# Graph-attention edge pass: VectorE's own semaphore against drains between its dependent instructions

## The reference

```python
def gat_layer(h, src, dst, W, al, ar, b):
    feat = (h @ W).reshape(n, H, F)                  # H = 4 heads, F = 64
    el = jnp.sum(feat * al[None], axis=-1)
    er = jnp.sum(feat * ar[None], axis=-1)
    e = jax.nn.leaky_relu(el[src] + er[dst], 0.2)
    m = jax.ops.segment_max(e, dst, num_segments=n)
    ex = jnp.exp(e - m[dst])
    denom = jax.ops.segment_sum(ex, dst, num_segments=n)
    a = ex / denom[dst]
    msg = feat[src] * a[:, :, None]
    out = jax.ops.segment_sum(msg, dst, num_segments=n)
    out = out + b.reshape(1, H, F)
    return jax.nn.elu(out).reshape(n, H * F)
```

## Time and profile before

| | |
|---|---|
| median of 3 runs | 8269.03 us (8267.43 to 8291.18) |
| the profiled execution | 8222.85 us |
| its span, first to last instruction | 8220.9 us |
| VectorE busy | 5315.2 us (65%), 9727 instructions |
| GpSimd busy | 5491.2 us (67%), 5324 instructions |
| ScalarE busy | 2245.6 us (27%) |
| TensorE matmuls busy | 2470.7 us (30%), almost none of it in `gat_edges` |

### The profile page before, as it was taken

How to read it: one execution, slowest core, us unless ns; L and a number is a source line. 1 busy time by engine, 2 the same in 40 slices (tenths; PEclk the granted TensorE clock), 3 DMA queues, 4 the chain that set the end, 5 groups by cost and what they waited for, 6 DMA issues and landing times. The chain is left out here.

```text
span 8220.9 us, 58166 instructions
## 1 busy us (share of the span) xinstructions
PE 2470.7 (30%) x11337; PEld 1689.0 (21%) x11337; DVE 5315.2 (65%) x9727; ACT 2245.6 (27%) x5114; POOL 5491.2 (67%) x5324
## 2 busy tenths in 40 slices
PE   4777777777667676000000000005100000000000
PEld 4444444444444455000000000004000000000000
DVE  6777777777768777556556655663456556655666
ACT  3667666767667552000000000002000000000002
POOL 4777777767777646666666666647766666666664
PEclk8888988888888798555555555557555555555555
DMA  7555555555555547555555555543455555555556
GB/s 240 162 167 164 167 163 167 168 160 170 160 160 168 157 135 217 166 189 196 184 197 179 201 180 198 185 170 93 140 191 190 191 195 182 197 182 200 176 207 220
DMA packets 680849, 1466.14 MB, mean 178 GB/s; under 512 B 164313, under 2 KB 497566, under 8 KB 667420
## 3 DMA queue, kind: packets, MB, share of 16 engines
q0 software_dynamic: 250192, 671.13, 28.1%
q1 hardware_dynamic: 430540, 793.82, 27.2%
HBM read 752.61 MB, written 713.36 MB: 178 GB/s over the span
## 5 line engine op out<-in xcount | busy, mean ns | idle before, releaser
L1810 POOL DMA_INDIRECT gb_g<-table,ix_g x3126 | 2965.2, 949 | 1442.6 <-issue 938.1
L585 POOL DMA_INDIRECT gb<-table,src x1563 | 1897.1, 1214 | 679.5 <-issue 468.9
L1910 DVE SCALAR_TENSOR_TENSOR gb_g<-gb_g,same_g,wv 128x256 f32<-128x256 f32 x3024 | 1450.0, 479 | 1135.8 <-DVE gb_g L1910 471.3
L1096 PE MATMUL pm<-ident,tl 128*4 128x128 f32 x2 | 0.7, 372 | 4531.2 <-DMA tl<-sums 4531.2
L619 PE MATMUL po<-parts,sel 128*128 128x256 f32 x3930 | 1026.0, 411 | 501.3 <-ACT ost L685 353.5
L1837 ACT ACTIVATE ww<-ee 128x132 f32<-128x132 f32 (+3 forms) x102 | 28.5, 280 | 4030.2 <-DVE ee L1888 2811.7
L1898 DVE TENSOR_TENSOR wv<-gb_g,ww 128x1024 f32<-128x1024 f32 x782 | 955.2, 1221 | 0.0
L1096 PEld LDWEIGHTS pm<-ident,tl 128*4 128x4 f32 x2 | 0.2, 81 | 4532.1 <-DMA tl<-sums 4532.1
L619 PEld LDWEIGHTS po<-parts,sel 128*128 128x128 f32 x3930 | 762.8, 202 | 746.5 <-issue 478.1
L762 DVE TENSOR_TENSOR pt<-gb,pt 128x256 f32<-128x256 f32 x392 | 175.8, 449 | 546.4 <-ACT pt L679 414.8
L679 ACT ACTIVATE pt<-pt,sh 128x128 f32<-128x128 f32 x1568 | 436.8, 344 | 331.8 <-remote 175.2
(11 more groups left out here) (302 smaller groups left out, 4208.3 us busy)
## 6 DMA issues: line engine op xcount, KB each, us to landing
sums<-gb_g SPq DMA_DIRECT2D x94, 4224.0 KB
sums<-ost SPq DMA_DIRECT2D x393, 512.0 KB
gb_g<-table,ix_g POOLq DMA_INDIRECT x3126
gb<-table,src POOLq DMA_INDIRECT x1563
table<-f SPq DMA_DIRECT2D x48, 520.0 KB
x<-in_x SPq DMA_DIRECT2D x50, 256.0 KB
at<-in_rbf SPq DMA_DIRECT2D x100, 128.0 KB
hT_d<-hT SPq DMA_DIRECT2D x49, 256.0 KB
```

The costliest lines, as they stand in the source:

```text
L585: eng.indirect_dma_start(out=gb[:, group(k), half(k) + j, 0:4, :].rearrange("p a c -> p (a c)"), out_offset=None, in_=q.table0[:, :], in_o ...
L1810: eng.indirect_dma_start(out=gb[:, p, j, 0:FR], out_offset=None, in_=q.table1[:, :], in_offset=bass.IndirectOffsetOnAxis(ap=ix[:, s * SBT ...
L1910: ins = eng.scalar_tensor_tensor(rows[:, t0 + t, 0:D], row, same[:, t:t + 1], wv[k % 2][:, j, :], ALU.mult, ALU.add)
```

## The change

`s_dv`, `own`, `after` and the clearing are gone. Where VectorE waited for its own count, it now has a `drain()`: an instruction of VectorE's sequencer that holds what follows until VectorE's earlier instructions are done. The wait for its own last row sum at a superblock's top becomes a drain too. All waits for other engines and for DMAs stay, and so do the updates that other engines wait for (`s_d`, `s_den`, `s_sum`).

```diff
-        s_dv = q.sem(nm("dv"))
...
-                def body(s, p, t0, t1, first, masks, arrived, before, behind, m_before):
+                def body(s, p, t0, t1, first, masks, arrived, behind, m_before):
                     m = t1 - t0
-                    made = 0
-
-                    def own(ins):
-                        nonlocal made
-                        made += 1
-                        ins.then_inc(s_dv, 1)
-                        return made
-
-                    def after(k):
-                        eng.wait_ge(s_dv, k)
-
...
-                    eng.wait_ge(s_sum.sem, before)
-                    eng.nop(nofuse=True)
-                    eng.sem_clear(s_dv)
+                    eng.drain()
                     eng.tensor_copy(same[:, 0:m], q.samep[:, here])
                     eng.wait_ge(s_seg.sem, s_seg.at(s, back=1))
                     eng.tensor_copy(lead(ee), carry(mm_))
                     eng.wait_ge(*arrived)
-                    k_el = own(eng.tensor_tensor(x, rows[:, t0:t1, D:FR].rearrange("p t h -> p h t"), held[:, :, here], ALU.add))
-                    after(k_el)
-                    k_el = own(eng.scalar_tensor_tensor(x, x, 0.2, x, ALU.mult, ALU.max))
-                    after(k_el)
-                    k_fs = own(eng.tensor_tensor_scan(line(fs, m), add_m, line(ee, m), -BIG, ALU.add, ALU.max))
-                    after(k_fs)
-                    k_mm = own(eng.tensor_tensor_scan(line(mm_, m)[:, ::-1], back_m, line(fs, m)[:, ::-1], -BIG, ALU.add, ALU.max))
-                    after(k_mm)
+                    eng.tensor_tensor(x, rows[:, t0:t1, D:FR].rearrange("p t h -> p h t"), held[:, :, here], ALU.add)
+                    eng.drain()
+                    eng.scalar_tensor_tensor(x, x, 0.2, x, ALU.mult, ALU.max)
+                    eng.drain()
+                    eng.tensor_tensor_scan(line(fs, m), add_m, line(ee, m), -BIG, ALU.add, ALU.max)
+                    eng.drain()
+                    eng.tensor_tensor_scan(line(mm_, m)[:, ::-1], back_m, line(fs, m)[:, ::-1], -BIG, ALU.add, ALU.max)
+                    eng.drain()
                     eng.tensor_tensor(heads(ee, m), heads(ee, m), heads(mm_, m), ALU.subtract).then_inc(s_d.sem, 1)
...
-                    k_w = own(weighted(0))
-                    after(k_w)
-                    k_dn = own(eng.tensor_tensor(lead(ww), lead(ww), carry(dn), ALU.mult))
-                    after(k_dn)
+                    weighted(0)
+                    eng.drain()
+                    eng.tensor_tensor(lead(ww), lead(ww), carry(dn), ALU.mult)
+                    eng.drain()
                     eng.tensor_tensor_scan(line(dn, m), mul_m, line(ww, m), 0.0, ALU.mult, ALU.add).then_inc(s_den.sem, 1)
-                    k_row = k_w
                     for t in range(m):
                         k, j = divmod(t, 4)
                         row = acc[:, :] if t == 0 else rows[:, t0 + t - 1, 0:D]
-                        after(k_row)
+                        eng.drain()
                         ins = eng.scalar_tensor_tensor(rows[:, t0 + t, 0:D], row, same[:, t:t + 1], wv[k % 2][:, j, :], ALU.mult, ALU.add)
                         if t == m - 1:
                             ins.then_inc(s_sum.sem, min(2, len(quads(t0, t1))))
-                        else:
-                            k_row = own(ins)
```

More of the change, by code:

```diff
@@ L1947, in whole @@
                     body(s, p, 0, SBT, s * SBT, [y[:, bass.ds(s * (H * W), H * W)] for y in (q.seg_add, q.seg_back, q.seg_mul)],
-                         (s_g[p].sem, s_g[p].at(i)), s_sum.at(s, 0), gb[:, (p - 1) % B, SBT - 1, 0:D], SBT)
+                         (s_g[p].sem, s_g[p].at(i)), gb[:, (p - 1) % B, SBT - 1, 0:D], SBT)
                 with eng.Fori(0, LOOPS) as i:
@@ L1958, in _ @@
                     body(SB - 2 + x, p, t0, t1, s * SBT + t0, [y[:, :] for y in end_masks[x]],
-                         (s_ge[x], 16 * (t1 - t0)), summed(x),
+                         (s_ge[x], 16 * (t1 - t0)),
                          gb[:, p, t0 - 1, 0:D] if t0 else gb[:, (p - 1) % B, SBT - 1, 0:D], ENDS[x - 1][2] - ENDS[x - 1][1] if x else SBT)
```

## The result

| | before | after |
|---|---|---|
| median of 4 runs each, on one chip | 8270.01 us (8267.43 to 8291.18) | 8440.61 us (8438.23 to 8449.05) |
| the profiled execution | 8222.85 us | 8440.26 us |
| from the first gather of a pass to its last row sum | 2250.4, 2248.2 us | 2338.2, 2340.7 us |

The ratio is 1.0207, 95% interval 1.0185 to 1.0228: the change makes the kernel **slower by some 170 us**. The forecast was 7715 us. The two passes alone are 88 + 92 = 180 us longer; the other 37 us between the two profiled executions lie ahead of them, in stages that the change doesn't touch (the profiled execution of before was the short one).

What follows compares the result with a forecast made beforehand. VectorE, at 44.9 us a superblock against GpSimd's 40.0, was taken as the bound. 8222.85 - 504 (GpSimd's waits) - 44 (the passes' ends) = 7675 us, put at 7715 for the median of the runs; range 7640 to 8030.

Steps and rivals of the forecast that it cites:

- GpSimd's 40.0 us: Edge passes: GpSimd needs 32 x 1.25 = 40.0 us a superblock when nobody holds it, and becomes the bound.
- VectorE's 28.9 us a clean superblock: Edge passes: VectorE would take 28.9 us a superblock with no late waits, which cost it 16 us.
- `wv` starts on time while dependents are late: VectorE's late regime: `wv`, which waits for nothing, starts on time; row sums stand 1.40 us apart, 0.92 us idle.
- The drains' own price: VectorE: 39 drains a superblock, a 0.12 us gap behind each in place of 0.035, add 4.2 us a superblock.
- the 33.1 of the sum: VectorE's superblock without late waits but with the drains' cost of 4.2 us added: 33.1 us.
- If what is late is the semaphore alone, all waits for itself are on time again: VectorE's waits for `s_dv`: a drain waits for earlier instructions, not a semaphore, so its 16 us a superblock of lateness largely go.
- the term - 504 us: Both edge passes: GpSimd's waits for VectorE's `wv`, 253.6 + 250.9 us, go.
- rival C: VectorE: completion itself is late and a drain sees it no sooner; + 200 to + 390 us, about 8550; chance 0.10.
- not under 400: Expected sign in the changed profile: VectorE's idle time before row sums falls from 1079 us to under 400.
- Its instructions end as before: VectorE's late regime: the engine isn't slow, row sums still last 0.48 us; only news of an end comes late.
- So VectorE sets the pace: Edge passes: VectorE bounds them at 44.9 us a superblock, since GpSimd waits for it and it hardly waits for gathers.
- C's boundary of 0.41 us a drain: If completion itself is late, the change loses above 16 us / 39 = 0.41 us a drain over today's good gap.

Runs made afterwards that it cites:

- the paced kernel: Kernel before, with a 128-column GpSimd memset behind each gather that first waits for the memset before it: 8251.78 us against 8309.21; repeated on another chip, ratio 0.9891.
- the paced kernel with drains: Changed kernel with a 128-column GpSimd memset behind each gather that first waits for the memset before it: 8260.84 us (kernel before, same chip: 8309.21).
- the paced kernels: A waiting GpSimd memset behind each gather: 16 or 128 columns in the kernel before, 128 in the changed one: 8263.46, 8251.78 and 8260.84 us against 8309.21.
- the first experiment: Changed kernel, each row sum reading `acc` and not the row before it, 23 of 32 drains ahead of row sums removed: 8416.44 us (kernel before: 8289.66).
- The kernel with breaks: Kernel before, with eight GpSimd memsets of 1500 columns behind every 16 gathers of the whole superblocks: 9903.21 us (kernel before, same chip: 8309.21).

## Why the prediction was wrong

*What held.* GpSimd's 40.0 us, VectorE's 28.9 us a clean superblock (a superblock of the paced kernel: 42.9 us from top to top, less 14.0 of waiting for gathers, is 28.9), and that `wv` starts on time while dependents are late. The drains' own price was taken too high: 31.4 us a superblock in the paced kernel with drains (45.6 less 14.2 of waiting) against the 33.1 of the sum. Had the late waits gone, VectorE would have had even more room than I gave it.

*The step that failed* is "If what is late is the semaphore alone, all waits for itself are on time again", and with it the term - 504 us. The condition was false. A drain lets go no sooner than a semaphore does, as rival C said: behind drains the late row sums stand 1.40 us apart, VectorE's idle time before them is 1105.5 us, not under 400, and GpSimd's waits grew by 79 and 84 us a pass in place of going. "Its instructions end as before" was read off a record of durations and an instruction that had nothing to wait for, and neither says when a wait learns that an instruction has ended. I had noted that `wv` doesn't rule this out and gave C 0.10 all the same, on one drain in a good stretch. A drain of 0.1 us there says nothing on a late stretch.

*A deeper step failed too:* "So VectorE sets the pace". Its lateness has a cause in GpSimd's gathers: without half of them, or with breaks in them, it is gone. Late stretches begin 29 to 43 us after GpSimd takes up its run of 64 gathers (median 33) and end mostly 6 to 10 us after it stops for a buffer, before the change and after it. As I read it, the two engines hold each other: gathers at 1.25 us make VectorE late, VectorE late keeps a buffer, GpSimd stops, and VectorE catches up. So to remove late waits is not to gain them: the paced kernels have lost most of their late row sums and still take 2225 to 2235 us a pass, at the 1.41 us a gather that the kernel before has on average too. The 40.0 us a superblock at which the prediction put GpSimd were never reached over a whole pass.

*Rival C's size.* It had + 200 to + 390 us and 8550; measured were + 170. It priced a superblock at 4.2 us more, where the drains add 2.5, and it let half the late steps swallow it. In fact all do: a late quad takes 7.00 us with or without drains. What is left for the drains is the good stretch. There VectorE falls behind, and GpSimd's stop lasts until it has caught up, 11.0 us becoming 14.4 on average: 23 stops x 3.4 = 78 us a pass, and the tail behind the last gather takes 52.7 us for 45.8. That is 85 of the 90 us. The 85 us are measured; that the longer good quad is why the stops grew is argued, from the table above, and the kernel with fewer drains speaks against its being the only reason. C's boundary of 0.41 us a drain had no meaning, since the late waits came back at any price.

*The rule* of the Trainium skill that I had weighed, in VectorE: DVE Perf Modes, on the drain that can't be avoided, says that a semaphore after each instruction costs nothing extra. By it nothing was to be gained from giving up `s_dv`, and I had added that the drains could only cost. That pointed to the right side. But the trace disagrees with its reason, in good stretches too: row sums that wait for nothing (the first experiment) take 1.25 us for three, 0.39 us apart, those behind a semaphore stand 0.52 us apart, and those behind a drain 0.555.

*Left open:* what holds a gather to 1.40 us, and how that makes a VectorE instruction's end late in steps of 0.70 us. It is not the stores, not the bytes, and not the gathers' data, which land in time. That the late time goes with the number of instructions, and that GpSimd's memsets are late too, points at something that the engines share when an instruction ends.

One candidate is the recording itself. Each gather adds 16 to its semaphore, and the trace should have an event for each. Just after GpSimd resumes it has 79 for 8 gathers (before, 4326 to 4336 us), in the late stretch behind it (4350 to 4400) 36 for 40. The kernel with breaks, which is hardly ever late, has some 300 for 30 throughout. So late stretches are those in which the trace loses most such events. Either the updates are in each other's way on the chip, or the profiler, which writes them down, slows the engines. The narrower gathers have as many updates as the full ones, so they don't tell. No execution without recording and no kernel with fewer updates at the same run of gathers is on record, so it isn't known whether these stretches are there when nobody records.

Open too are the waits of 3.7 to 4.5 us at a superblock's top. In each run that has them the queue of kind instruction moved 1.25 to 1.93 MB (1.34 in the changed kernel), in each other one 0.73 to 0.93, so they go with that queue's traffic; I take it for the fetching of instructions, which isn't tested. The 31 NOPs more in the loop don't bring them, and the pass that has them is no longer than the other.

## What to carry to other kernels

Before the cause of a wait is taken for its mechanism, look at what else on the chip begins and ends with the late stretches: here they followed another engine's run of gathers, with a lag of some 30 us, and none of the edits to VectorE's own waits removed them. Look also whether other engines' ends are late at the same time; here GpSimd's were. Where dependent instructions of one engine are ordered, a semaphore is at least as cheap as a drain, most of all behind a long instruction into which the next could have run. And holding back an engine that runs ahead only to stop can pay: a memset behind each gather, with a wait for the one before, brought 1.1%.

## What the runs showed of the hardware

- In an unbroken run of indirect gathers at 1.25 us, from some 30 us on, the ends of VectorE's instructions reach its own drains and semaphores late, mostly in steps of 0.70 us (waits of 0.23, 0.92, 1.6 and 2.2 us). A drain and a semaphore in a row cost the delay once. (See above: the recording may have a part in it.) Broken up by breaks of 11 us, the gathers bring hardly any of it.
- In such stretches five instructions of VectorE take 7.00 us (6.3 to 7.0 when held once), nine take 11.2 us and more. NOPs of the sequencer don't count.
- GpSimd's own memsets are late in the same way: an update 1.85 us behind the end, beside 128-column memsets.
- In good stretches the explicit drain costs 0.04 us more than a semaphore wait behind a short instruction, and 0.18 us behind `wv`, where the waiting row sum used to start 0.09 us before `wv` had ended.
- VectorE's copy of 128x4 numbers takes 0.17 us, but beside GpSimd's memsets of 1500 columns (the kernel with breaks) 92 of 102 take 1.85 us in the median, and the ten that meet no memset 0.16, while row sums keep their 0.48:

```profile
L1891 DVE COPY ee<-mm x102: 153/1846/1961, 3383.0 to 9720.0; 128x4 f32<-128x4 f32 x102
```
